# Moving the last shared expert quarter's down products of layer 0 into the attention of layer 1

## The reference, cut to what matters

```python
x = x + xattn0(layernorm(x), ctx)
x = x + ffn0(layernorm(x))      # 64 experts, 8 per token, and a shared expert
x = x + xattn1(layernorm(x), ctx)
x = x + ffn1(layernorm(x))      # 32 experts, 6 per token, a shared expert, 16 anchors
# shared expert of ffn0, h = layernorm(x):
shared = silu(h @ W_gate) * (h @ W_up) @ W_down     # 512 inner features
x = x + sigmoid(h @ w_s) * shared + routed
```

## Time and profile before

| | us |
|---|---|
| median of three runs | 967.52 |
| the profiled execution | 971.25 |
| its span, first to last instruction | 969.5 |
| PE busy | 834.7 (86%) |
| DVE busy | 653.1 (67%) |
| ACT busy | 487.7 (50%) |
| POOL busy | 541.5 (56%) |

### The profile page before, as it was taken

How to read it: one execution, slowest core, us unless ns; L and a number is a source line. 1 busy time by engine, 2 the same in 40 slices (tenths; PEclk the granted TensorE clock), 3 DMA queues, 4 the chain that set the end, 5 groups by cost and what they waited for, 6 DMA issues and landing times. The chain is left out here.

```text
span 969.5 us, 23162 instructions
## 1 busy us (share of the span) xinstructions
PE 834.7 (86%) x6360; PEld 644.8 (67%) x6360; DVE 653.1 (67%) x3241; ACT 487.7 (50%) x1602; POOL 541.5 (56%) x531
## 2 busy tenths in 40 slices
PE   5798888868899999978998997788699999999850
PEld 3566666654588789556776775556577888888730
DVE  3678888654255555366899999786356666666597
ACT  3677777753033343336766665312345555555520
POOL 1006666777367777596055557673655666656630
PEclk9899999889999999998999999789899999999965
DMA  9964421107799997652012242896588555554596
GB/s 319 344 212 172 175 76 60 48 16 269 237 276 319 316 302 118 119 195 88 2 73 91 85 150 108 336 371 214 184 258 288 171 160 154 163 161 138 155 413 236
DMA packets 112991, 183.47 MB, mean 189 GB/s; under 512 B 18631, under 2 KB 86809, under 8 KB 111842
## 3 DMA queue, kind: packets, MB, share of 16 engines
q1 hardware_dynamic: 76194, 122.02, 38.1%
q0 software_dynamic: 29088, 50.52, 18.1%
q10 hardware_dynamic: 7584, 9.45, 3.0%
HBM read 106.38 MB, written 90.86 MB: 203 GB/s over the span
## 5 line engine op out<-in xcount | busy, mean ns | idle before, releaser
L1009 POOL DMA_INDIRECT buf<-R,RI x240 | 235.8, 983 | 218.0 <-ACT R L1177 105.9
L799 PE MATMUL PS<-R,XT 128*128 x632 | 152.6, 365 | 10.9 <-DVE XT L1645 10.9
L325 PE MATMUL PS<-R 128*128 128x256 f32 (+2 forms) x352 | 110.0, 443 | 12.2 <-DMA R<-in_ctxT 10.2
L1645 DVE COPY XT<-PS 128x256 f32<-128x256 f32 x222 | 94.0, 423 | 38.8 <-PE PS L330 36.4
L799 PEld LDWEIGHTS PS<-R,XT 128*128 128x128 f32 x632 | 104.6, 194 | 19.1 <-issue 12.4
L1352 ACT ACTIVATE SL<-PS 128x128 f32<-128x128 f32 (+1 forms) x158 | 42.2, 267 | 110.7 <-PE PS L799 107.8
L1177 ACT ACTIVATE R<-R,MX 128x120 f32<-128x120 f32 x256 | 80.1, 387 | 32.7 <-DVE MX L1467 32.7
L325 PEld LDWEIGHTS PS<-R 128*128 128x128 f32 (+1 forms) x352 | 64.1, 200 | 41.8 <-issue 33.3
L1177 ACT ACTIVATE R<-PS,MX 128x120 f32<-128x120 f32 x256 | 71.5, 367 | 38.9 <-DVE MX L1467 38.9
L1935 DVE TENSOR_TENSOR AC<-SL,PS 128x128 f32<-128x128 f32 (+1 forms) x158 | 43.3, 274 | 61.8 <-ACT SL L1352 60.4
L1044 POOL DMA_INDIRECT yb<-YT,DI x65 | 63.3, 973 | 34.3 <-DVE DI L1635 28.5
(11 more groups left out here) (218 smaller groups left out, 1928.7 us busy)
## 6 DMA issues: line engine op xcount, KB each, us to landing
R<-in_ew SPq DMA_DIRECT2D x64, 384.0 KB, 5.7
BX<-buf SPq DMA_DIRECT2D x128, 140.0 KB
R<-buf SPq DMA_DIRECT2D x94, 140.0 KB
R<-in_w SPq DMA_DIRECT2D x8, 1536.0 KB, 15.1
R<-yb SPq DMA_DIRECT2D x8, 1536.0 KB, 20.9
buf<-Z SPq DMA_DIRECT2D x8, 1120.0 KB, 13.6
yb<-Z SPq DMA_DIRECT2D x17, 512.0 KB, 3.3
R<-yb SPq DMA_DIRECT2D x16, 512.0 KB, 3.5
```

Of the source, the lines that this page charges most:

```text
L325: m = e.matmul(out_, left, right, start=(i == 0), stop=(i == len(pairs) - 1))
L799: x = e.matmul(PS[:, 2 + j % 2, 0:2 * wd], XT[:, j % 3, k, :], src[:, bass.ds(regs[j], 1), k * 2 * wd:(k + 1) * 2 * wd].rearrange("p a n - ...
L1009: e.indirect_dma_start(out=(buf1 if l else buf0)[:, :], out_offset=bass.IndirectOffsetOnAxis(ap=RI[:, n % 6, k:k + 1].bitcast(U32), axis=0 ...
L1645: e.tensor_copy(XT[:, j % 3, :, :], two(PS[:, j % 2, 0:256])).then_inc(S["d_xt"], 1)
```

## The change

The gate and up products of group 3 stay where they are. The four down products leave this place: they go into the attention of layer 1 as the generator `first` on PE, at slots 23, 35, 47 and 59 after its start (units 0, 2, 4 and 6), and DVE adds them at slots 26, 38, 50 and 62 (units 1, 3, 5 and 7). Their results use the two turning banks. Their weights were in the region of `R` that the attention overwrites, so SP loads a second copy of the down weights (512 KB) into the tile `BX` when the expert loop of layer 0 is done with it; `bx1_load` waits for `s_dn` 32 before it uses `BX` again.

In the prologue of layer 1 both halves of the keys go first on PE and on ACT, ahead of the rows of block 0. The wait of PE for all additions goes. Tile 2 of `y_add` moves from DVE to POOL. POOL's additions to tiles 12 to 15 wait, as before, for the 16th addition of `add0`, which now comes in unit 7.

```diff
+        SD0B = BX[:, :, :].rearrange("p s n -> p (s n)")[:, 0:1024].rearrange("p (c n) -> p c n", c=4)
...
-            elif n in (0, 2):
-                w.wait_ge("d_xc", n // 2 + 1)
+            elif n == 0:
+                w.wait_ge("d_xc", 1)
             else:
-                w.wait_ge("p_xc", 1 if n == 1 else n - 1)
+                w.wait_ge("p_xc", n)
...
-                    w.wait_ge("d_as", 16)
+                    w.wait_ge("d_as", 15)
+                    w.wait_ge("d_add", 4 * BESIDE)
...
                 keys_out(0)
+                if l:
+                    w.wait_ge("d_as", 16)
+                    keys_out(1)
                 for i in range(2):
                     rows_in(0, i)
-                keys_out(1)
+                if l == 0:
+                    keys_out(1)
...
-                if l:
-                    w.wait_ge("d_add", 16)
-                else:
+                if l == 0:
                     turns.append(2)
                     reader[2] = "a_kt", 8
+
+                def last_downs():
+                    yield from pause(23)
+                    for j in range(4):
+                        n = 4 * BESIDE + j
+                        w.wait_ge("l_sd", 16)
+                        mm(e, bank("dn", n, sem="d_add", n=n + 1),
+                           [(AS_[:, i, j * P:j * P + P], SD0B[:, i, :]) for i in range(4)]).then_inc(S["s_dn"], 1)
+                        yield from pause(12)
...
-                sweep(l, main, prepare, finish, None, behind + ([tables()] if l else []))
+                sweep(l, main, prepare, finish, last_downs() if l else None, behind + ([tables()] if l else []))
...
+            for i in range(4):
+                k, rhs = 4 * BESIDE + i, [H2T[:, c, BESIDE * 512:BESIDE * 512 + 512] for c in range(2)]
+                w.wait_ge("d_as", k - 1)
+                mm(e, PS[:, 2 * (k % 2), :], [(SG0L[:, c, i * P:i * P + P], rhs[c]) for c in range(2)])
+                mm(e, PS[:, 2 * (k % 2) + 1, :], [(SG0L[:, c, 512 + i * P:512 + i * P + P], rhs[c]) for c in range(2)]).then_inc(
+                    S["s_gu"], 1)
...
+            w.wait_ge("s_ta", E0)
+            w.wait_ge("d_wc", E0)
+            e.dma_start(SD0B, chunks("sd0")).then_inc(S["l_sd"], 16)
...
                     w.wait_ge("z_dum", 32)
+                    w.wait_ge("s_dn", 32)
...
-                    if n not in (0, 2):
+                    if n:
...
+                if l:
+                    for half in range(2):
+                        keys_in(half, 0)
+                        keys_in(half, 1)
                 spread(0)
-                keys_in(0, 0)
-                if l:
-                    keys_in(0, 1)
+                if l == 0:
+                    keys_in(0, 0)
...
+                def last_adds():
+                    yield from pause(26)
+                    for n in range(4 * BESIDE, NT):
+                        w.wait_ge("s_dn", n + 1)
+                        add0_from(n, misc(1, "dn", n))
+                        yield from pause(12)
...
             last_gated(3)
-            y_add(2)
-            for j in range(4):
-                w.wait_ge("s_dn", 4 * BESIDE + j + 1)
-                add0(4 * BESIDE + j, (4, 6)[j % 2])
```

More of the change, by code:

```diff
@@ L131 @@
 SIGNALS = (
-    ["l_c", "l_ct", "l_mask", "l_wr0", "l_s0", "l_small", "out"]
+    ["l_c", "l_ct", "l_mask", "l_wr0", "l_s0", "l_sd", "l_small", "out"]
     + [f"l_x{i}" for i in range(4)] + ["l_" + n for n in WNAMES]
@@ L919, in yl_loads @@
                 waits_x(w, 1, 0)
-                waits_x(w, 1, 2)
                 waits_x(w, 1, NT - 1)
@@ L1140, in queries_in @@
                                      scale=0.25).then_inc(S["a_q"], 1)
+                if l:
+                    for half in range(2):
+                        keys_in(half, 0)
+                        keys_in(half, 1)
                 spread(0)
-                keys_in(0, 0)
-                if l:
-                    keys_in(0, 1)
+                if l == 0:
+                    keys_in(0, 0)
                 for i in range(2):
                     rows_in(0, i)
-                keys_in(1, 0)
-                if l:
-                    keys_in(1, 1)
+                if l == 0:
+                    keys_in(1, 0)
                 for c in range(2):
@@ L1522, in main @@
                             divide((u - 3) // 2)
-                sweep(l, main, prepare, finish, None, behind)
+                def last_adds():
[4 more added lines that the diff above has]
+                        yield from pause(12)
+                sweep(l, main, prepare, finish, last_adds() if l else None, behind)
             def shared(l, nchunk, ready, add, groups):
@@ L1607, in add0, with add0_from @@
             def add0(n, bank):
-                e.scalar_tensor_tensor(out=X[:, n, :], in0=PS[:, bank, 0:256], scalar=SIG[:, n:n + 1], in1=X[:, n, :],
+                add0_from(n, PS[:, bank, 0:256])
+            def add0_from(n, down):
+                e.scalar_tensor_tensor(out=X[:, n, :], in0=down, scalar=SIG[:, n:n + 1], in1=X[:, n, :],
                                        op0=ALU.mult, op1=ALU.add).then_inc(S["d_add"], 1)
```

## The result

The changed kernel takes 973.13 us (median of 11 runs, 971.41 to 977.25). The kernel before takes 967.52 us (11 runs, 965.30 to 970.28). The medians differ by 5.6 us, where 4.6 was forecast. The ratio of the runs is 1.0071, 95% interval 1.0057 to 1.0085, which is 6.9 us (5.5 to 8.2), so 5.6 is at the lower end of what was measured. The profiled execution after took 971.65 us.

The account below looks back on a forecast made before the run. Bounds: an entry chain, PE to 470.2 us, then DVE, then POOL at the next expert loop. -5.5 + 5.4 + 0.5 + 0.5 + 0.5 + 3.2 = +4.6 us on 967.52, so 972.1 us, range 965 to 977.

Parts of the forecast that it names:

- What bounds each stage: Attention of layer 1: a chain at the entry, PE from 441.5 to 470.2 us, DVE from about 470; then POOL.
- The entry: Start of the attention: without the down products in the chain, the first maximum comes 5.5 us earlier, bounds -6.5 and -3.6.
- Rival E: Entry: tile 1's statistics or routed rows come late, block 0 as late as before; about 0, 967.5 us; chance 0.07.
- Three products on PE: Down products 0 to 2, in the stretch where PE is full, cost 3 x 1.79 = 5.4 us.
- Rival C: Early units: PE has holes, so the down products cost it nothing; -5.0 us, 962.5 us; chance 0.10.
- The fourth product and the addition: Product 3, after the value products at 470.2, costs 0.5 us; DVE's fourth addition, in unit 7, costs 0.5 us.
- POOL's late additions: Tiles 12 to 15: POOL's twelve instructions beside a full DVE at 473 to 485 us lengthen DVE's; +3.2 us.
- Rival B: Unit 7 on: POOL's late additions cost DVE next to nothing; +1.4 us, 968.9 us; chance 0.22.
- The clock: Entry: PE at half speed delays queries, scores and values; +0.5 us, bounds 0 and 3.5.
- rival D: The clock falls at the entry and the POOL-DVE lock is held in full; +8.8 us, 976.3 us; chance 0.13.
- Edits at nothing: Second weights copy, tile 2 on POOL, wait of `bx1_load`: costed at 0, the wait hidden by PE's 6.96 us standstill.
- The sum: Whole kernel: all terms together +4.6 us, 972.1 us for the median, as forecast A; chance 0.48.

Follow-up runs that it names:

- x3: Changed kernel with three quarters of each of the four moved down products left out; 0.9981 of the kernel before, last wait ends at 68.18 us instead of 71.90.
- x1: Kernel before with only POOL's last additions to tiles 12 to 15 made late; whole time +0.2% and +0.1% in two runs, scatter 4.0 us late.
- x4: Changed kernel with ACT's two normalising activations after its first two key activations instead of all eight; 0.9966 of the kernel before (0.9911 to 1.0020).
- z1: Repeat run of the changed kernel with POOL's additions to tiles 12 to 15 early again; scatter at 91.38 us instead of 95.71 on the same chip.
- y2: Changed kernel with the first loads of layer 1's expert rows waiting for the 16th down product, not the 32nd; 1.0023 of the kernel before.
- y0: The changed kernel itself, run again on another chip; 1.0062 of the kernel before.
- y1: Changed kernel with POOL's additions early, ACT's normalisation ahead and three down products in PE's idle time; 0.9883 of the kernel before, scatter at 83.2 us.
- x2: First run of the changed kernel with POOL's additions to tiles 12 to 15 early again; 19.6 us from last wait to scatter, instead of 23.5.

## Why the prediction was nearly right, step by step

- **What bounds each stage:** confirmed. PE is full in units 1 to 6, DVE from unit 7 on; x3 and x1 show that what is added to either there is paid in full.
- **The entry:** forecast -5.5, measured -6.17, within its bounds. Keys on PE at 410.15 (forecast 411.8), ACT's normalisation at 417.14 (419), both near once the earlier start of 1.9 us is taken off. That ACT would be late next is shown by x4. Rival E (block 0 as late as before) fails with this.
- **Three products on PE:** forecast 3 x 1.79 = 5.4. The trace gives 6.17 - 1.58 = 4.6 for everything in the stretch, and x3 gives 5.0 to 5.2 for the products alone. The first took 2.78 us, its larger part at half the clock, but the clock then rose ahead of the work that ran at half before, which gave 1.7 us back. My 3 x 1.79 left both out. Rival C fails here: PE has no hole from 437.0 to 466.7.
- **The fourth product and the addition:** forecast 0.5 + 0.5. The addition took 0.47 us. Its neighbourhood also brought a DVE wait of 0.51 us for ACT before 471.34, which I had not seen. I can't separate the fourth product.
- **POOL's late additions, the term that decides:** forecast 3.2, measured 3.6 in the changed kernel (the lengthened DVE instructions summed) and 4.2 alone in x1, within the bounds 0 to 5.5. The mechanism was right: one POOL instruction holds DVE up once, and maxima and reads of PS are spared. The mean was right too: 0.46 us forecast, 0.45 and 0.52 measured. What was a little short is the count: 3.2 us is seven meetings, and there were eight, with ten instructions of POOL, for two of the twelve had run before the wait. Single losses lie between 0.10 and 0.82 us, according to what was left of POOL's instruction. Rival B fails. By the Trainium skill ("SBUF — State Buffer", section "SBUF: two separate sides"), the lock holds for the instruction's whole length and touches only DVE instructions with two SBUF inputs or in a mode with both ports. The trace agrees on which are hit (copies, casts and scalings from SBUF and products of two small SBUF tensors, not PS reads nor MAX8), and on the length in so far as the eight end with POOL's instruction; the unstretched instruction at 422.87 that the prediction names is against it. The 5 to 6 us that the prediction estimated from it were more than was paid.
- **The clock:** forecast 0.5 at the entry, with bounds 0 and 3.5. The profiled run has no fall there, but one at 480 us that came from DVE's delay, which the prediction had not foreseen. From the scaling of `EW` to the scatter it takes 0.55 us longer, and by the values of block 4 another 1.0 us is lost to PE: together some 1.6 us. z1 shows that both come from POOL's late additions. How much of it is the clock and how much PE's wait of 2.11 us is argued, not isolated by a run. In x1 the fall came later (544 us); it cost nothing by the scatter and some 0.4 us behind it. The other chips show that the fall that rival D supposes does come in 3 of 8 executions, at 2.1 to 2.7 us. I took the mean of something that comes or doesn't.
- **Edits at nothing:** the wait of `bx1_load` is hidden (y2), and the standstill got 1.98 us shorter where 1 was forecast. Tile 2 on POOL and the second copy of the weights left no wait that counts in the entry: DVE waits 1.23 us for POOL's tile 1 at 412.22, but then 4.21 us for ACT.
- **The sum:** forecast +4.6. The profile shows +3.55 at the scatter, +4.57 from the values of block 4 on, and +3.34 at the memset; the runs show +5.6 by the medians and +6.9 by the ratio. In terms: -6.17 for the entry, +4.59 up to the last wait, +0.47 for the addition, +0.51 for the wait on ACT, +3.6 for the lock, +1.6 for PE behind it, which is +4.6. If the entry's clock fell as often in the timed runs (3 in 8 of some 2.4 us), that is 0.9 us more, less what such falls cost the kernel before. This is argued, not shown, and 1 to 3 us between the profile and the runs stay open.

So the number was nearly right, by terms that erred both ways: entry 0.7 better, the stretch with the three products 0.8 better, lock 0.4 to 1.0 worse, and some 1.6 us at PE where 0.5 stood for another place. That they cancel to 4.6 is luck; the mechanisms of entry, products and lock are not. The prediction also gave "the same" (up to 972.4 us) 0.56 and "slower" 0.37; with an interval of 0.14% on either side the change is clearly slower, and 973.13 lies above that bound.

## What to carry to other kernels

A step moved from a chain into a stage where its engine is full is no gain in itself: look for the holes of the engine first, and move it there (of the 12.6 us between y0 and y1, some 4.3 are POOL's additions and 1.5 ACT's order by their own runs; the other 6.7, clock included, are left for the place of the products, which no run isolates). Follow what waits for the moved step to the engines that seem to have spare time: POOL's additions, hidden before, cost DVE 3.6 to 4.2 us once they ran beside it while it was full, and some 5 us with what PE lost behind it. Count such a collision meeting by meeting, the smallest instructions too: each meeting costs the rest of the other engine's instruction, and the busy engine then makes others late.

## What was not expected of the hardware

- Beside POOL's additions, DVE instructions of a few elements lose more than they last, since they end with the POOL instruction that they meet, however short they are: 128x2 0.63 us for 0.16, 128x6 0.71 for 0.17, 128x4 0.92 for 0.17, cast of 128x6 0.97 for 0.16. Instructions of the same kinds on 128x1 (0.14 us at 477.50) slipped between two of POOL's. In all eight traces with late additions the same eight instructions are hit, with the same lengths within 0.03 us but for the normalisation (0.65 or 1.23 us).
- After a wait of 2.11 us PE's clock was at half for some 6 us more, though PE was then fully busy. In the kernel before, PE had no such wait near there and stayed at full.
- The fall at the entry came in some executions of one and the same stream and not in others (x2 and z1 are the same kernel: 36.52 and 34.29 us to the first maximum).
